# Graph layer, sums by destination: one 112-node window per chunk becomes two 64-node windows, one for each part of 13 and 12 tiles, with weights read 128 columns wide

## The chip, the cores and the metric

The kernel runs on one core of one Trainium2 chip. The metric is the device time of one execution in microseconds (us). Smaller is better. Engine names below are those of the profile: PE is TensorE's matmul, PEld its weight load, DVE is VectorE, ACT is ScalarE, POOL is GpSimd, SP is SyncE, whose queue (SPq) issues most of the transfers.

## The reference

There are 12,500 nodes with 16 features and 400,000 edges, sorted by destination. Each layer adds to x something gathered over the edges, and then normalises:

```python
inv_dx = 1.0 / jnp.maximum(edge_attr_2[:, 0], 1e-6)
slope_e = edge_attr_2[:, 1] * inv_dx
diff = (u[dst] - u[src]) * inv_dx[:, None]
d1 = segment_sum(diff, dst, N) - segment_sum(diff, src, N)
S = segment_sum(broadcast(slope_e, 16), dst, N)
u_next = u - clip(dt, 0.01, 2.0) * (u * d1 + g * S)
x = layernorm(x + u_next)
x = layernorm(x + segment_sum(edge_attr_16, dst, N) / max(count_by_dst, 1))
```

The node ids src and dst are drawn uniformly, and the edges are then sorted by dst, so that a node has 32 edges on the mean (400,000 / 12,500).

## The kernel before, in words

The edges are cut into C = 125 chunks of CH = 3200 edges, each chunk in J = 25 tiles of P = 128 edges. A transfer puts edge 25p + j of a chunk on partition p, as tile j, so that every tile holds edges from the whole of the chunk's span of destinations. That span is about 100 nodes. A window of WIN = 112 nodes from the chunk's least dst holds it. For a chunk with a wider span there is a loop over further windows (`further_in`), which is entered when a table says so; no instruction of its body is in this trace.

Each chunk needs three kinds of TensorE work:

- Sums by src (`tile`, L667 to L678). For every tile the weights are the payload, split in two halves (k) and spread over 8 low positions, and the moving data is a one-hot over 1563 high positions, in four banks (392, 392, 392 and 387 columns). This is 200 matmuls a chunk, L657 and L662, accumulated over all chunks in `ps_src`.
- Rows of x for dst (`take_row`, L599). For every tile one matmul of 48 columns, with the one-hot `node_of_dst` as weights (112 partitions, 128 columns).
- Sums by dst (`take_sum`, L610). For every tile one matmul: weights are the tile's 102 columns of `parts` (3 bf16 parts of 34 values), the moving data is the tile's one-hot of 112 columns, `dst_of_node`, and all 25 accumulate in columns 0 to 111 of `ps_w`.

TensorE runs one stage for each chunk c. Among the matmuls of the 25 tiles of c, the order written by hand puts the rows of x for chunk c + 2 (from tile ROWS_AT = 6, one after each half) and the sums by dst of chunk c + 1 (from tile SUM_AT = 11 to 19, alternately one and two after a half). At tile 11 it waits for `parts_ready`, which DVE gives after L926.

DVE runs one stage for each chunk as well. It opens with `load_stage` (values of the stage's windows from a table into registers) and `add_window` (L962), which waits for the last sum by dst, adds `ps_w` to `dst_sum` at the chunk's base (L971) and copies `dst_rel` to `more_rel` (L972). Then come 25 one-hots of 1564 columns (L1018), and between them the pieces that prepare the next chunk: L929 (`dst_rel2`, the destinations less the chunk's base, doubled), five one-hots of 5 tiles x 112 columns (L939), the arithmetic of the payload (L897 to L926), the spread (L997). One-hots lie in a ring of 13.

ACT builds `node_of_dst` from `rel_all` (L537, L539) and casts. POOL gathers x[src] with one indirect transfer for each tile (L436), paced by TensorE's progress. SP reloads src, dst, the two edge attributes, the window of x and `rel_all` for later chunks, six transfers a stage, each behind a semaphore that frees its buffer.

Before the first stage a prologue finds each chunk's least and greatest dst on DVE (L793, L800), writes the relative destinations to `rel_d` (L798), makes the tables through three small matmuls (L584 to L586), and takes rows and sums of chunk 0 outside the stages. After the last stage the sums are turned and the layers are finished.

Of the kernel before, what the change touches and what calls it, by code (L numbers as in the profile page):

```python
# [5 lines left out]
def gnn_kernel(nc, x, src, dst, edge_attr_16, edge_attr_2, dt_in, g_in, out):  # L6
# [7 lines left out]
    P = 128  # L14
# [14 lines left out]
    WIN = 112  # L29
    SPL = 3  # L30
# [14 lines left out]
    assert NODES <= 1 << 14 and WIN == 16 * 7  # L45
# [6 lines left out]
    src_v = src.rearrange("(c p j) -> c p j", p=P, j=J)  # L52
    dst_v = dst.rearrange("(c p j) -> c p j", p=P, j=J)
    a2_v = edge_attr_2.rearrange("(c p j) t -> c p (j t)", p=P, j=J)
    a16_v = edge_attr_16.rearrange("(c p j) f -> c p (j f)", p=P, j=J)

    ctx = ExitStack()
    with ctx:
# [24 lines left out]
        dst_of_node = dst_hots[:, 0:J * WIN].rearrange("p (j e) -> p j e", j=J)  # L83
# [14 lines left out]
        parts = sb("parts", [P, J, SPL, V], bf16)  # L98
# [25 lines left out]
        more_i = sb("more_i", [P, 2], i32)  # L124
        more_f = sb("more_f", [P, 1], f32)
        base_diag = sb("base_diag", [P, P], f32)
        base_all = sb("base_all", [P, P], f32)
        base_tab = sb("base_tab", [1, P], i32)
        more_tab = sb("more_tab", [1, P], i32)
        stage_tab = sb("stage_tab", [1, (C + 1) * 4], i32)  # L130
# [117 lines left out]
        def later(base, g, first):  # L248

            return nc.s_assert_within(base + (g - first + 1) * WIN, 0, NODES - 1,  # L250
                                      skip_runtime_bounds_check_because="windows are counted up to the one that holds the greatest dst")

        def further_span(eng, c):

            return nc.values_load_multi_w_load_instructions(more_tab[0:1, ds(c, 2)], engines=[eng.engine], min_val=0, max_val=C * (NODES // WIN))[1]

# [56 lines left out]
        A_STEPS, B_STEPS, W_STEPS = 2, 20, 1  # L313
# [8 lines left out]
        def _(sp):  # L322
            def load_src(c, b):
                sp.dma_start(src_i[:, b, :], src_v[ds(c, 1), :, :].rearrange("o p j -> (o p) j")).then_inc(src_loaded[b], 16)

            def load_dst(c, b):
                sp.dma_start(dst_i[:, b, :], dst_v[ds(c, 1), :, :].rearrange("o p j -> (o p) j")).then_inc(dst_loaded[b], 16)

            def load_a2(c, b):
                sp.dma_start(a2[:, b, :], a2_v[ds(c, 1), :, :].rearrange("o p j -> (o p) j")).then_inc(a2_loaded[b], 16)  # L330
# [23 lines left out]
            sp.wait_ge(rel_ready, 1)  # L354
# [64 lines left out]
        def _(pool):  # L419
# [5 lines left out]
            def gather(k, b, pace=None, first=None):  # L425

                pool.wait_ge(src_loaded[b], k * 16 + 16)
# [31 lines left out]
        def _(act):  # L459
# [19 lines left out]
            act.wait_ge(dst_max_ready, 1)  # L479
# [42 lines left out]
            def attr_parts(m, k, b, first=False):  # L522

                act.wait_ge(a16_loaded[b], k * 16 + 16)
# [55 lines left out]
        def _(pe):  # L580
# [4 lines left out]
            nc.tensor.matmul(ps_w[0:1, P:P + C + 1], more_f[0:C, :], before[0:C, 0:C + 1], start=True, stop=True)  # L585
            nc.tensor.matmul(ps_w[:, 2 * P:2 * P + C], ones[0:C, :], base_diag[0:C, 0:C], start=True, stop=True).then_inc(tab_sum, 1)  # L586
# [26 lines left out]
            def sums(hots):  # L613
                for j in range(J):
                    last = take_sum(hots, j)
                return last
# [7 lines left out]
            def further_rows(n):  # L624
# [11 lines left out]
                return span  # L636

            def window_sums(n, span, first=False):

                pe.wait_ge(dst_hot_ready, n + 1)  # L640
                pe.wait_ge(parts_ready, n + 1)
                if not first:
                    pe.wait_ge(win_added, n)
                sums(dst_of_node).then_inc(win_sum_ready, 1)
                further_sums(span)

            def further_sums(span):

                def more(g, first):
                    pe.wait_ge(more_dhot, g + 1)  # L650
                    sums(more_node).then_inc(more_sum, 1)

                further_in(pe, span, more)
# [13 lines left out]
            def tile(c, j, stop, does_sums, does_rows):  # L667
# [4 lines left out]
                for k in range(HLV):  # L672
# [8 lines left out]
                    for s in range((j - SUM_AT) * 3 + first, (j - SUM_AT) * 3 + first + count):  # L681
                        if does_sums and 0 <= s < J:
                            one = take_sum(dst_of_node, s)
# [46 lines left out]
            span = further_rows(0)  # L730
# [3 lines left out]
            window_sums(0, span, first=True)  # L734
# [15 lines left out]
        def _(dve):  # L750
# [7 lines left out]
            def settle(base=0):  # L758
# [15 lines left out]
            step(v.memset(parts[:, :, :, :], 0.0))  # L774
# [18 lines left out]
            step(v.tensor_reduce(lim[0:C, 0:1], dst_all, AX, ALU.min))  # L793
# [4 lines left out]
            v.tensor_scalar(rel_split.rearrange("c (j p) -> c j p", p=P), dst_all.rearrange("c (p j) -> c j p", j=J),  # L798
                            lim[0:C, 0:1], None, ALU.subtract).then_inc(rel_ready, 1)
            v.tensor_reduce(lim[0:C, 1:2], dst_all, AX, ALU.max).then_inc(dst_max_ready, 1)  # L800
            dve.wait_ge(dst_max_ready, 1)
            step(v.tensor_tensor(more_i[0:C, 0:1], lim[0:C, 1:2], lim[0:C, 0:1], ALU.subtract))
            step(v.tensor_scalar(base_diag[0:C, 0:C], ident[0:C, 0:C], lim[0:C, 0:1], None, ALU.mult))
            settle()

            step(v.tensor_single_scalar(more_i[0:C, 1:2], more_i[0:C, 0:1], 4, ALU.arith_shift_right))
            settle()
            step(v.tensor_single_scalar(more_i[0:C, 0:1], more_i[0:C, 1:2], 9363, ALU.mult))
            settle()
            step(v.tensor_single_scalar(more_i[0:C, 1:2], more_i[0:C, 0:1], 16, ALU.arith_shift_right))  # L810
            settle()
            v.tensor_copy(more_f[0:C, :], more_i[0:C, 1:2]).then_inc(tab_sum, 1)
            dve.wait_ge(tab_sum, 2)
            step(v.tensor_copy(base_tab[0:1, 0:C], ps_w[0:1, 0:C]))
            step(v.tensor_copy(more_tab[0:1, 0:C + 1], ps_w[0:1, P:P + C + 1]))
            settle()
            v.tensor_copy(base_all[:, 0:C], ps_w[:, 2 * P:2 * P + C]).then_inc(tables_ready, 1)
            dve.wait_ge(tables_ready, 1)
            by_stage = stage_tab[:, :].rearrange("o (s q) -> o q s", q=4)
            step(v.tensor_copy(by_stage[:, 0, 1:C + 1], more_tab[0:1, 0:C]))  # L820
            step(v.tensor_copy(by_stage[:, 1, 0:C + 1], more_tab[0:1, 0:C + 1]))
            step(v.tensor_copy(by_stage[:, 2, 0:C], more_tab[0:1, 1:C + 1]))
            step(v.tensor_copy(by_stage[:, 3, 1:C + 1], base_tab[0:1, 0:C]))
# [11 lines left out]
            def load_stage(s):  # L835

                before_last, last, after, base = nc.values_load_multi_w_load_instructions(
                    stage_tab[0:1, ds(s * 4, 4)], engines=[dve.engine], min_val=0, max_val=max(C * (NODES // WIN), NODES - 1))[1]
                done["window"] = (before_last, last)
                done["span"] = (last, after)  # L840
                done["base"] = base

            def finish(n, k, b, piece, base_step):
# [36 lines left out]
                if piece == "lo":  # L880
                    if isinstance(n, int) and n == 0:
                        dve.wait_ge(src_loaded[0], 16)
# [294 lines left out]
```

## Time and profile before

| what | value |
|---|---|
| median of 3 runs | 4494.73 us |
| lowest and highest of them | 4491.13 and 4495.12 us |
| the profiled execution's own time | 4491.46 us |
| its span, first to last instruction | 4489.6 us |
| PE busy | 4396.0 us, 98% |
| DVE busy | 3896.7 us, 87% |
| POOL busy | 3316.7 us, 74% |
| ACT busy | 1431.9 us, 32% |
| mean granted clock of TensorE | 0.996 of 2.4 GHz |

The span is the time between the first and the last instruction on the core; the execution's own time is 1.9 us longer. A matmul's busy time in the profile is from its start to the arrival of its last result, and neighbours overlap, so what a matmul costs in a dense stream is read from the distance between starts, not from its own duration. An engine that is not the bound may idle without cost.

### The profile page before, as it was taken

To read this page: it belongs to the slowest core of one execution; us is meant where nothing else is said; L and a number is where in the kernel's file an instruction comes from. 1 tells how busy PE (TensorE), PEld (TensorE's weight loads), DVE (VectorE), ACT (ScalarE), POOL (GpSimd) and SP (SyncE) were. 2 spreads that over 40 slices of the span, in tenths; PEclk is the share of its full clock that TensorE was granted. 3 is DMA by queue.
4 is the path that set the end of the run, shared out by engine and by line. 5 is a ranking of instruction groups with operands and counts; after the bars stand their busy time and mean duration, and the time that the engine had idled before them with its cause. 6 is when DMAs were issued, how large, how long until landed. Compare 5 with 4: busy or idle time off the path is not lost. (4 is left out here: it accounts for less than half of the span.)

```text
span 4489.6 us, 74222 instructions
## 1 busy us (share of the span) xinstructions
PE 4396.0 (98%) x31379; PEld 1159.0 (26%) x12630; DVE 3896.7 (87%) x8730; ACT 1431.9 (32%) x1018; POOL 3316.7 (74%) x3133
## 2 busy tenths in 40 slices
PE   4999999999999999999999999999999999999997
PEld 1222222222222222222222222222222222222222
DVE  7988888888888888888888888888888888888887
ACT  4333333333333333333333333333333333333320
POOL 7777777777777777777777777777777777777760
PEclk9999999999999999999999999999999999999998
DMA  3111111111111111111111111111111111111110
GB/s 94 35 35 35 43 37 35 35 35 42 37 35 35 36 42 37 35 35 41 39 35 35 35 43 37 35 35 35 43 37 35 35 35 42 37 35 35 36 31 8
DMA packets 210292, 167.80 MB, mean 37 GB/s; under 512 B 124651, under 2 KB 193775, under 8 KB 210025
## 3 DMA queue, kind: packets, MB, share of 16 engines
q1 hardware_dynamic: 109798, 139.79, 9.9%
q0 software_dynamic: 100000, 25.80, 6.6%
q10 hardware_dynamic: 476, 2.01, 0.1%
q8 instruction: 7, 0.11, 0.0%
q14 instruction: 11, 0.08, 0.0%
HBM read 164.55 MB, written 2.81 MB: 37 GB/s over the span
## 5 line engine op out<-in xcount | busy, mean ns | idle before, releaser
L662 PE MATMUL ps_src<-hi_hot,spread_lo 128*128 128x392 bf16 (+1 forms) x18750 | 4114.8, 328 | 0.0
L436 POOL DMA_INDIRECT x_src<-in_x_dram,src_i x3125 | 3311.7, 1060 | 1039.9 <-issue 906.0
L1018 DVE TENSOR_SCALAR hi_hot<-col_h,hi_f,scale 128x1564 bf16<-128x1564 f16 x3125 | 2161.3, 711 | 24.4 <-PE ps_src L662 23.2
L657 PE MATMUL ps_src<-hi_hot,spread_lo 128*128 128x392 bf16 x6250 | 2048.4, 328 | 11.4 <-DVE hi_hot L1018 9.3
L657 PEld LDWEIGHTS ps_src<-hi_hot,spread_lo 128*128 128x128 f16 x6250 | 616.0, 99 | 1718.2 <-issue 1383.6
L537 ACT ACTIVATE nodes_mem<-rel_all,row_neg 128x3200 bf16<-128x3200 f16 x125 | 370.3, 2962 | 1507.1 <-PE ps_x L599 1505.0
L610 PEld LDWEIGHTS ps_w<-dst_hots,parts 128*102 128x102 bf16 x3125 | 391.3, 126 | 939.4 <-issue 901.4
L997 DVE TENSOR_TENSOR spread_lo<-spread_lo,halves 128x640 f16<-128x640 f16 x1250 | 603.3, 491 | 12.6 <-PE ps_src L662 12.4
L599 PE MATMUL ps_x<-xwin,nodes_mem 112*128 112x48 bf16 x3125 | 579.9, 188 | 20.4 <-DVE parts L926 13.5
L610 PE MATMUL ps_w<-dst_hots,parts 128*102 128x112 bf16 x3125 | 499.5, 213 | 0.0
L599 PEld LDWEIGHTS ps_x<-xwin,nodes_mem 112*128 112x128 bf16 x3125 | 302.4, 98 | 601.2 <-issue 563.5
L971 DVE TENSOR_TENSOR dst_sum<-dst_sum,ps_w 102x112 f32 x125 | 34.0, 272 | 475.1 <-PE ps_w L610 475.1
L539 ACT ACTIVATE nodes_mem<-nodes_mem,ones 128x3200 bf16<-128x3200 bf16 x125 | 370.3, 2962 | 4.1
L520 ACT COPY spread_lo<-lo_hot 128x3200 f16<-128x3200 f16 x124 | 353.8, 2853 | 0.0
L939 DVE TENSOR_TENSOR dst_hots<-col_h,dst_rel 128x560 bf16<-128x560 f16 x625 | 275.6, 442 | 0.0
L515 ACT CAST halves<-ps_x 128x400 f16<-128x400 f32 x125 | 61.5, 492 | 668.9 <-DVE ps_x L914 668.9
L529 ACT CAST parts<-attr_rest 128x400 bf16<-128x400 f32 x125 | 71.3, 570 | 516.5 <-DVE attr_rest L959 516.5
L830 DVE TENSOR_REDUCE ps_w<-ps_x 128x160 f32<-128x480 f32 x375 | 191.8, 570 | 0.4 <-DVE dst_rel L1005 0.4
L517 ACT CAST parts<-ps_x 128x425 bf16<-128x425 f32 x125 | 68.1, 545 | 126.8 <-DVE ps_x L917 126.8
L511 ACT CAST parts<-ps_w 128x425 bf16<-128x425 f32 x125 | 68.2, 546 | 109.1 <-DVE ps_w L900 109.1
L897 DVE TENSOR_TENSOR ps_w<-ps_w,x_src 128x400 f32<-128x400 f32 x125 | 70.8, 567 | 10.6 <-DMA x_src<-in_x_dram,src_i 10.6
L926 DVE TENSOR_TENSOR parts<-ps_x,parts 128x425 bf16<-128x425 f32 x125 | 75.3, 603 | 4.3
(120 smaller groups left out, 1164.2 us busy)
## 6 DMA issues: line engine op xcount, KB each, us to landing
rel_all<-rel_d SPq DMA_DIRECT2D x125, 800.0 KB
x_src<-in_x_dram,src_i POOLq DMA_INDIRECT x3125
a<-in_edge_attr_dram SPq DMA_DIRECT2D x125, 200.0 KB, 2.4
a<-in_edge_attr_dram SPq DMA_DIRECT2D x125, 25.0 KB
src_i<-in_src_dram SPq DMA_DIRECT2D x125, 12.5 KB, 1.7
dst_i<-in_dst_dram SPq DMA_DIRECT2D x125, 12.5 KB, 1.7
xwin<-xparts_d SPq DMA_DIRECT2D x125, 10.5 KB
dst_sum<-in_dst_dram SPq DMA_DIRECT2D x1, 1400.0 KB
```

Source lines behind the costliest of these rows:

```text
L436: nc.gpsimd.indirect_dma_start(x_src[:, b, j * F:(j + 1) * F], None, x[:, :], bass.IndirectOffsetOnAxis(ap=src_i[:, b, j:j + 1], axis=0)). ...
L520: nc.scalar.copy(lo_rows[:, :, :, :], bc(lo_hot[:, :, :], 3, F)).then_inc(lo_rows_ready, 1)
L537: nc.scalar.activation(node_of_dst[:, :, :], rel_all[:, :, :], ACT.Abs, bias=row_neg[:, 0:1], scale=1.0).then_inc(node_diff_ready, 1)
L539: nc.scalar.activation(node_of_dst[:, :, :], node_of_dst[:, :, :], ACT.Relu, bias=ones[:, 0:1], scale=-1.0).then_inc(node_hot_ready, 1)
L599: return nc.tensor.matmul(ps_x[:, j // PER, (j % PER) * SPL * F:(j % PER + 1) * SPL * F], nodes[0:WIN, j, :], window, start=True, stop=True)
L610: return nc.tensor.matmul(ps_w[0:SPL * V, 0:WIN], parts[:, j, :, :].rearrange("p k v -> p (k v)"), hots[:, j, :], start=(j == 0), stop=(j ...
L657: return nc.tensor.matmul(out_bank, weights, moving, start=False, stop=stop)
L662: return nc.tensor.add_instruction(mybir.InstMatmult(name=nc.get_next_instruction_name(), engine=pe.engine, start_tensor_calc=False, stop_ ...
L830: yield v.tensor_reduce(out_t[:, q * PER:q * PER + n, :], ps_x[:, q, 0:n * SPL * F].rearrange("p (j k f) -> p j f k", k=SPL, f=F), AX, ALU ...
L939: ins = v.tensor_tensor(dst_of_node[:, five, :].rearrange("p j (n t) -> p j n t", t=2), bc(col_h[:, 0:WIN].rearrange("p (n t) -> p n t", t ...
L997: ins = v.tensor_tensor(spread[:, tiles, q, :, :], lo_rows[:, tiles, :, :], bc(halves[:, tiles, q, :], 2, LO), ALU.mult)
L1018: v.tensor_scalar(hi_hot[:, slot(j), 0:HOT], col_h[:, 0:HOT], hi_f[:, b, j:j + 1], scale[:, b, j:j + 1], ALU.is_equal, ALU.mult).then_inc( ...
```

## The change

Edges are laid out differently. A chunk's first 13 x 128 = 1664 edges are part 0 and its last 12 x 128 = 1536 are part 1; within a part of n tiles, edge n·p + j goes to partition p, tile j. So the four loads of a chunk's edge data are two transfers each, and their semaphores count 32 in place of 16. Each part's destinations are counted from the part's own least dst, one-hots by dst have 64 columns in place of 112, and the sums of part 0 go to columns 0 to 63 and of part 1 to columns 64 to 127 of `ps_w`. The weights of a sum are 128 consecutive columns of `parts_mem`, that is the tile's 102 and 26 of what lies behind them; the results of these 26 are not used. DVE adds two windows of 64 in place of one of 112. If a part spans 64 nodes or more, the chunk's further loop runs with destinations outside the parts' windows; it has a table of its own, `sum_tab`.

```diff
+    PWIN = 64
+    JA = 13
+    PARTS = [(0, JA), (JA, J)]
...
+        PARTW = SPL * V
+        parts_mem = sb("parts_mem", [P, J * PARTW + P - PARTW], bf16)
...
             def load_a16(c, b):
-                sp.dma_start(a16[:, b, :], a16_v[ds(c, 1), :, :].rearrange("o p j -> (o p) j")).then_inc(a16_loaded[b], 16)
+                for lo, hi in PARTS:
+                    sp.dma_start(a16[:, b, lo * F:hi * F], part_of(a16_v, c, lo, hi, F)).then_inc(a16_loaded[b], 16)
...
-            def take_sum(hots, j):
-                return nc.tensor.matmul(ps_w[0:SPL * V, 0:WIN], parts[:, j, :, :].rearrange("p k v -> p (k v)"),
-                                        hots[:, j, :], start=(j == 0), stop=(j == J - 1))
+            def part_weights(j):
+                return parts_mem[:, j * PARTW:j * PARTW + P]
+            def take_sum(j):
+                part = int(j >= JA)
+                lo, hi = PARTS[part]
+                return nc.tensor.matmul(ps_w[:, part * PWIN:(part + 1) * PWIN], part_weights(j), dst_of_node[:, j, :],
+                                        start=(j == lo), stop=(j == hi - 1))
...
                 if finish:
-                    span = further_rows(c + 1)
+                    further_rows(c + 1)
+                    span = further_span(pe, c + 1, sum_tab)
...
                 if piece == "rel2":
-                    step(v.tensor_copy(dst_rel2[:, :, :], bc(dst_rel[:, b, :], 2, 2)))
+                    for part, (lo, hi) in enumerate(PARTS):
+                        step(v.tensor_scalar(dst_rel2[:, lo:hi, :], bc(dst_rel[:, b, lo:hi], 2, 2), bases_all[:, 1 + part, ds(n, 1)], None, ALU.subtract))
...
-                win = dst_sum[0:SPL * V, ds(base, WIN)]
-                v.tensor_tensor(win, win, ps_w[0:SPL * V, 0:WIN], ALU.add).then_inc(win_added, 1)
-                step(v.tensor_scalar(more_rel[:, :], dst_rel[:, b, :], 0.0, None, ALU.add))
+                step(v.tensor_tensor(win_a, win_a, ps_w[0:PARTW, 0:PWIN], ALU.add))
+                step(v.tensor_scalar(far[:, :], dst_rel2[:, :, 0], float(PWIN), float(FAR), ALU.is_lt, ALU.mult))
+                dve.wait_ge(dve_step, base_step + count[0])
+                v.tensor_tensor(win_b, win_b, ps_w[0:PARTW, PWIN:2 * PWIN], ALU.add).then_inc(win_added, 1)
+                step(v.tensor_tensor(more_rel[:, :], dst_rel[:, b, :], far[:, :], ALU.add))
```

Besides, `load_stage` takes seven values in place of four. In the prologue the least and the greatest dst are each found for two parts and combined, `rel_split` is written in two instructions, some ten small DVE instructions make the parts' bases and the second table, and the small matmuls that make the tables are more. The initial loads of chunks 0 and 1 are in two transfers each as well, the first of them ahead of `dst_all`, from which the least dst is taken.

## Rows read from the trace of the kernel before

**Rows 1.** The page: busy time and share of PE, and the granted clock in tenths.

```profile
PE 4396.0 (98%) x31379; PEld 1159.0 (26%) x12630; DVE 3896.7 (87%) x8730; ACT 1431.9 (32%) x1018; POOL 3316.7 (74%) x3133
...
PEclk9999999999999999999999999999999999999998
```

**Rows 2.** What PE waited for: us in total, times, longest us.

```profile
PE ps_x L599 <- DVE parts L926: 13.5, 1, 13.5
PE ps_src L657 <- DVE hi_hot L1018: 9.3, 4, 5.8
```

**Rows 3.** Groups by form, PE and PEld: count, busy us, mean ns, idle before.

```profile
L599 PE MATMUL ps_x<-xwin,nodes_mem 112*128 112x48 bf16 x3125 | 579.9, 188 | 20.4 <-DVE parts L926 13.5 <-ACT nodes_mem L539 6.9
L610 PE MATMUL ps_w<-dst_hots,parts 128*102 128x112 bf16 x3125 | 499.5, 213 | 0.0
...
L657 PEld LDWEIGHTS ps_src<-hi_hot,spread_lo 128*128 128x128 f16 x6250 | 616.0, 99 | 1718.2 <-issue 1383.6 <-DVE hi_hot L1018 248.4
L610 PEld LDWEIGHTS ps_w<-dst_hots,parts 128*102 128x102 bf16 x3125 | 391.3, 126 | 939.4 <-issue 901.4
L599 PEld LDWEIGHTS ps_x<-xwin,nodes_mem 112*128 112x128 bf16 x3125 | 302.4, 98 | 601.2 <-issue 563.5
```

**Rows 4.** Timeline of PE, one stage's length: start us, length us, instruction, count.

```profile
2003.65 0.19 PE L599 MATMUL ps_x<-xwin,nodes_mem 112*128 112x48 bf16 x1
...
2010.54 0.21 PE L610 MATMUL ps_w<-dst_hots,parts 128*102 128x112 bf16 x1
...
2011.28 0.26 PE L610 MATMUL ps_w<-dst_hots,parts 128*102 128x112 bf16 x2
...
2021.95 0.26 PE L610 MATMUL ps_w<-dst_hots,parts 128*102 128x112 bf16 x2
...
2023.42 0.33 PE L657 MATMUL ps_src<-hi_hot,spread_lo 128*128 128x392 bf16 x1
...
2038.64 0.19 PE L599 MATMUL ps_x<-xwin,nodes_mem 112*128 112x48 bf16 x1
```

**Rows 5.** Timeline of DVE around a stage's start, idle before in brackets.

```profile
2007.51 0.60 DVE L926 TENSOR_TENSOR parts<-ps_x,parts 128x425 bf16<-128x425 f32 x1
...
2023.06 0.27 DVE L971 TENSOR_TENSOR dst_sum<-dst_sum,ps_w 102x112 f32 x1 [3.80 <-PE ps_w L610]
2023.25 0.17 DVE L972 TENSOR_SCALAR more_rel<-dst_rel 128x25 f32<-128x25 f32 x1
2023.63 1.88 DVE L1018 TENSOR_SCALAR hi_hot<-col_h,hi_f,scale 128x1564 bf16<-128x1564 f16 x3 [0.20 <-PE ps_src L662]
...
2028.40 0.19 DVE L929 CAST dst_rel<-dst_rel 128x50 f16<-128x50 f32 x1
```

**Rows 6.** Timeline of the prologue, several engines.

```profile
0.73 0.41 SPq L324 DMA_DIRECT2D src_i<-in_src_dram  x1
...
13.61 3.49 DVE L793 TENSOR_REDUCE lim<-dst_sum 125x1 f32<-125x3200 int32 x1 [2.90 <-DMA dst_sum<-in_dst_dram]
...
18.74 5.94 DVE L798 TENSOR_SCALAR fin_mem<-dst_sum,lim 125x3200 f16<-125x3200 int32 x1
...
39.63 0.57 DVE L959 TENSOR_TENSOR attr_rest<-a,parts 128x400 f32<-128x400 f32 x1 [6.10 <-ACT parts L527]
...
40.35 1.89 DVE L939 TENSOR_TENSOR dst_hots<-col_h,dst_rel 128x560 bf16<-128x560 f16 x5
...
53.85 1.25 PE L599 MATMUL ps_x<-xwin,nodes_mem 112*128 112x48 bf16 x25 [13.51 <-DVE parts L926]
54.92 2.56 PE L610 MATMUL ps_w<-dst_hots,parts 128*102 128x112 bf16 x25
```

**Rows 7.** POOL's gathers on the page, and their waits for PE.

```profile
L436 POOL DMA_INDIRECT x_src<-in_x_dram,src_i x3125 | 3311.7, 1060 | 1039.9 <-issue 906.0
...
POOL x_src L436 <- PE ps_src L662: 130.3, 239, 3.2
```

**Rows 8.** The longest wait of SP's queue, and one of its transfers.

```profile
SPq L339 <- PE ps_x L599: 1420.6, 124, 21.9
...
2032.04 0.33 SPq L333 DMA_DIRECT2D a<-in_edge_attr_dram  x1
```

More of the change, by code:

```diff
@@ L584, in _ @@
             nc.tensor.matmul(ps_w[0:1, 0:C], lim[0:C, 0:1], ident[0:C, 0:C], start=True, stop=True)
-            nc.tensor.matmul(ps_w[0:1, P:P + C + 1], more_f[0:C, :], before[0:C, 0:C + 1], start=True, stop=True)
-            nc.tensor.matmul(ps_w[:, 2 * P:2 * P + C], ones[0:C, :], base_diag[0:C, 0:C], start=True, stop=True).then_inc(tab_sum, 1)
+            nc.tensor.matmul(ps_w[0:1, P:P + C + 1], more_f[0:C, 0:1], before[0:C, 0:C + 1], start=True, stop=True)
+            nc.tensor.matmul(ps_w[0:1, 2 * P:2 * P + C + 1], more_f[0:C, 1:2], before[0:C, 0:C + 1], start=True, stop=True)
+            for part in range(2):
+                nc.tensor.matmul(ps_x[0:1, 0, part * P:part * P + C], part_lim[0:C, part:part + 1], ident[0:C, 0:C], start=True, stop=True)
+            for t in range(3):
+                last = nc.tensor.matmul(ps_x[:, 1, t * P:t * P + C], ones[0:C, :], base_diag[0:C, t, 0:C], start=True, stop=True)
+            last.then_inc(tab_sum, 1)
             pe.wait_ge(gi_done, 3)
@@ L635, in further_rows, with window_sums_first @@
                 further_in(pe, span, more)
[L636 to L645, printed above, removed]
+            def window_sums_first():
+                pe.wait_ge(dst_hot_ready, 1)
+                pe.wait_ge(parts_ready, 1)
+                for j in range(J):
+                    last = take_sum(j)
+                last.then_inc(win_sum_ready, 1)
+                further_sums(further_span(pe, 0, sum_tab))
             def further_sums(span):
@@ L733, in _ @@
             x_of_dst(1)
-            window_sums(0, span, first=True)
+            window_sums_first()
             with pe.Fori(0, C - 2) as i:
@@ L773, in _ @@
             v.memset(more_rel[:, :], 0.0).then_inc(more_b, 1)
-            step(v.memset(parts[:, :, :, :], 0.0))
+            step(v.memset(parts_mem[:, :], 0.0))
             dve.wait_ge(gi_done, 3)
@@ L792, in _ @@
             dve.wait_ge(dst_all_loaded, 32)
-            step(v.tensor_reduce(lim[0:C, 0:1], dst_all, AX, ALU.min))
+            for part, (lo, hi) in enumerate(PARTS):
+                step(v.tensor_reduce(part_lim[0:C, part:part + 1], dst_all[:, lo * P:hi * P], AX, ALU.min))
+            settle()
+            step(v.tensor_tensor(lim[0:C, 0:1], part_lim[0:C, 0:1], part_lim[0:C, 1:2], ALU.min))
             dve.wait_ge(xrest_ready, 1)
@@ L835, in load_stage @@
             def load_stage(s):
[L837 to L840, printed above, removed]
+                sums_first, sums_last, rows_first, rows_last, base, base_a, base_b = nc.values_load_multi_w_load_instructions(
+                    stage_tab[0:1, ds(s * QS, QS - 1)], engines=[dve.engine], min_val=0, max_val=max(C * (NODES // WIN + 1), NODES - 1))[1]
+                done["window"] = (sums_first, sums_last)
+                done["span"] = (rows_first, rows_last)
                 done["base"] = base
+                done["part_bases"] = (base_a, base_b)
             def finish(n, k, b, piece, base_step):
```

136 lines of the change are left out of this document (86 added, 50 removed).

## The prediction, made before the change was run

> **What bounds the kernel now.** I read the page first. PE is busy 98% of the span at the full granted clock, 2.4 GHz, in all but the ends of it [rows 1]. A busy PE is not yet a PE that sets the time, so the next view is what it waited for. Its two longest waits for DVE in or before the stages are 13.5 us once, in the prologue, and 9.3 us in four pieces [rows 2]. Over 124 stages that is nothing: inside a stage no other engine holds PE. The reader should then see in the timeline of PE that a stage takes 2038.64 - 2003.65 = 34.99 us, and that its matmuls follow each other without a hole [rows 4]. 125 x 34.99 is 4374 us of the 4489.6. So a nanosecond taken out of PE's stream in a stage is a nanosecond of the result, until some other engine becomes the slower one.
>
> **What each kind of matmul costs in the stream.** Durations overlap, so I take distances between starts, over long stretches so that the rounding to 10 ns goes away [rows 4].
> - From 2023.42 to 2038.64 there are only halves of tiles, four wide matmuls each, 23 of them: 15.22 / 23 = 0.6617 us each.
> - From 2003.65 to 2010.54 there are 10 halves with one row matmul (48 columns) each: 6.89 / 10 = 0.689 us. A row matmul costs 27.3 ns.
> - From 2010.54 to 2021.95 there are 15 halves, 15 row matmuls and 22 sums (eight halves with one, seven with two): 11.41 - 15 x 0.6617 - 15 x 0.0273 = 1.075 us, over 22 is 48.8 ns for a sum of 112 columns.
> Check: 50 x 0.6617 + 25 x 0.0273 + 25 x 0.0488 = 34.99 us, the stage. 112 columns at 2.4 GHz are 46.7 ns, so a sum pays for its columns and 2.2 ns more, and its 102-column weight load lies under the neighbours. A row matmul with 48 columns would be 20 + 2.2 = 22.2 ns but costs 27.3, so there is a floor near 27 ns for a pair of load and matmul.
>
> **The change on PE.** A sum has 64 columns: 26.7 + 2.2 = 28.9 ns, just above the row's 27.3. That needs a weight load that fits under 29 ns. The load of 102 columns takes 126 ns from start to end, the 128-column loads of L657 and L599 take 99 and 98 [rows 3]: the wider load is the shorter. If both have the same fixed part, the difference, 27 ns, is in the columns. And the 128-column kind does run at 27.3 ns a pair, in the rows. In the prologue, with PE after a long idle time, 25 rows take (1.25 - 0.19) / 24 = 44 ns each while 25 sums take (2.56 - 0.21) / 24 = 98 ns each [rows 3, 6], which is 112 columns at 1.2 GHz (93 ns) and a little. So I take 29 ns as the price of the new sum. Bounds: 27.3 ns (the row's) from below, 48.8 ns from above if the load stays what a 102-column load may be and only fits under as much as now. A stage has 25 sums, 124 stages have them: 3100 x (48.8 - 29) = 61.4 us saved. At 27.3 it would be 66.7 us; at 48.8 nothing.
>
> The Trainium skill, "TensorE: Matmul & The Clock Gate", sections "Weight-path perf modes" and "Back-to-back issue gap", says that weights are read in the fast way exactly when they are 128 columns and not fp32, and that a matmul of 1 to 64 columns has a floor of about 60 cycles, 25 ns. The 98 and 99 against 126 ns agree with the first, the 27.3 ns of the rows lies 2 ns above the second. By the floor of 25 ns the saving would be 73.8 us. The same page's section "LDWEIGHTS" speaks against the change: a load is put at its columns divided by 1.2 GHz, 107 ns for 128. If that were the slot of a sum, the change would cost 3100 x (107 - 48.8) = 180 us. The trace does not agree: by that rule the 102 columns of now would take 85 ns, and a sum's slot is 48.8.
>
> **PE's other additions.** Two more values are loaded from `sum_tab` in PE's queue at each stage's start. Before, two loads and a branch stand at the same place and there is no hole there: the 23 halves between 2023.42 and 2038.64 include the end of one stage and the start of the next at the same 0.6617 us [rows 4]. The queue runs ahead of the array. I cost it at nothing; cover gone, each 100 ns of hole is 12.4 us.
>
> **DVE.** The window: L971 to L972 is 0.19 us and L972 0.17 [rows 5]. Two adds of 64 for one of 112, one small instruction more and a wait for it: between 0.2 and 0.55 us more, I take 0.35. L929 becomes two: 0.1 to 0.2 more [rows 5]. The five one-hots of 560 elements follow each other at (1.89 - 0.44) / 4 = 0.36 us [rows 6]; with 320 elements at least 0.21, I take 0.24, so 5 x 0.12 = 0.6 us less (between 0 and 0.75). Net about -0.1 us, at worst +0.75. Seven values for four are loaded while DVE idles: it waits 3.80 us for the last sum in every stage [rows 5]. What remains after the stage shrinks by 25 x 19.8 ns = 0.50 us is 3.80 - 0.50 + 0.1 = 3.4 us, at worst 2.5. The point where PE could first feel DVE is tile 11, behind `parts_ready`: L926 ends at 2008.11 and PE gets there at 2010.54, 2.4 us later [rows 4, 5]. No one-hot or payload step moves by more than 0.75 us, so it holds. POOL, ACT and PE behind these DVE steps have the same margins or more. I cost DVE at nothing.
>
> **SP and the transfers.** Ten issues a stage for six, at 0.33 us each: 1.3 us more in a queue that waits 1420.6 us for PE alone, 11.4 us a stage [rows 8]. Every load is for a chunk one to two stages later. Nothing on the path.
>
> **POOL.** This is the engine with the least room. Its own time for 3125 gathers is 3311.7 + 906.0 = 4217.7 us, 33.74 us a chunk, and it waits 130.3 us for PE, 1.04 a chunk [rows 7]. The stage falls to 34.99 - 0.50 = 34.49 us, still 0.75 above POOL.
>
> **Ends of the program.** On the path before the first stage are SP's one extra issue ahead of `dst_all` (0.4 us), L793 and L798 each cut in two with one combining step (0.4), and the window of chunk 0 (0.35) [rows 5, 6]. The small steps for the tables run before 39.63, where DVE has idled 6.10 us for ACT [rows 6]; some ten steps of 0.15 to 0.3 us fit. The 25 sums at the low clock fall from 98 to about 64 / 1.2 + 5 = 58 ns: -1.0 us. At the last stage another 0.3. Together +0.5 us; bounds -1 to +4.
>
> **Sum.** 4491.46 (the profiled execution) - 61.4 + 0.5 = 4430.6 us. The profiled execution lies 3.3 us under the median of the runs shown and near the lowest, so I put 2.4 of it back: **4433 us**, 1.4% less. Its own range is 4426 to 4440. A difference of 0.2%, 9 us, is about what a measurement of this kernel can tell from no change.
>
> **Rivals.**
> 1. The sum costs more than its columns. The 64-column sum gets a slot between 33 and 46 ns because a load cannot be put under so short a neighbour where two sums stand together, or because weights that begin at steps of 204 bytes, as these do, load less well. For it: no 128-column load of this kernel begins off a 256-byte step. Against it: the row's 27.3 ns. At 40 ns: 3100 x 8.8 = 27 us saved, 4467 us. Chance 8%.
> 2. Slower, by one mechanism: the 128-column load of `parts_mem` isn't the fast kind. Then 128 columns at the rate at which the 102 would go through, 53.3 + 2.2 = 55.5 ns, set the slot in place of the 64 columns, 6.7 ns more than now, 3100 x 6.7 = +21 us: 4516 us. It decides as soon as a slot is over 48.8 ns. For it, again the odd start of the weights, and 26 columns that belong to the next tile; against it, 98 and 99 ns for the other two 128-column loads, of both partition counts and both 2-byte types [rows 3]. Chance 6%.
> 3. A new wait in each stage. POOL slows by more than 0.75 us a chunk, since eight loads of 128 short rows share the transfer engines with it where four did, or a changed mix on DVE holds it up, and PE then waits for x[src] through DVE's L897; or PE's queue shows a hole at the stage's start. Half the gain eaten is 0.25 us a stage: 4464 us. Against it: 3.80 us of DVE idle, 0.75 us of POOL room and a buffer of most of a stage between a gather and its reader. Chance 8%, of which 2 in the hundred are so large that the kernel is no faster.
> 4. A part spans 64 nodes or more, so that the further loop runs. A part of 1664 edges at 32 a node spans about 53 nodes, and the spread of that is little over one node. Chance 1%.
>
> **Chances and range.** The forecast has 77%. Faster by over 0.2%: 77 + 8 + 6 = 0.91, less what could lie at the small end, 0.89. Within 0.2%: 0.03. Slower: 0.08 with the second rival, the worst of the third and the fourth. The range for 8 in 10 takes the forecast's own range and the near part of the first and third rivals: 4426 to 4448 us.
>
> **What the profile would show.** L610's starts in a pair 29 ns apart and its loads at 98 ns with 128 columns; a stage of 34.49 us between two like places; DVE's idle before the window add at 3.3 to 3.5 us; POOL's waits for PE down from 130 to about 70 us; PE without waits in the stages; L939 with 320 elements near 0.3 us. It is wrong if a pair of sums stands 33 ns or more apart, if PE waits in every stage, or if loads of `parts_mem` take 126 ns or more.

## The result, and the profile after

The forecast was 4433 us. The changed kernel takes 4585.79 us (median; 4581.80 to 4589.75), the kernel before beside it 4492.47 us: ratio 1.0207, interval 1.0196 to 1.0218. It is slower by 93 us where 59 us less was expected (4492.5 - 4433), so 153 us have to be explained. The chance that I gave to slower was 0.08.

The page after: busy times, the granted clock, the queue that brings instructions (packets, MB, share), and three groups.

```profile
PE 4370.4 (95%) x31389; PEld 1042.3 (23%) x12640; DVE 3847.9 (84%) x9123; ACT 1438.9 (31%) x1018; POOL 3340.3 (73%) x3133
...
PEclk9999999999999999999999999999999999999998
...
q14 instruction: 311, 2.55, 0.2%
...
L641 PEld LDWEIGHTS ps_w<-dst_hots,parts_mem 128*128 128x128 bf16 x3125 | 302.9, 98 | 964.8 <-issue 898.9
...
L641 PE MATMUL ps_w<-dst_hots,parts_mem 128*128 128x64 bf16 x3125 | 436.7, 193 | 0.0
```

The clock is what it was [rows 1], so the loss is not there. PE fell from 98% to 95% of the span, and DVE from 87% to 84%: both idle more. The sum's load takes 98 ns with 128 columns where 102 took 126 [rows 3], as forecast. One line is new in kind. The page before has this one for the same queue:

```profile
q14 instruction: 11, 0.08, 0.0%
```

311 packets against 11 are 300 more, five in each of 60 or so passes through DVE's loop. A pass is one run through the loop's body, which holds two stages.

Timeline of PE after, the 25 sums of a stage (first rows, the last pair, the last):

```profile
2020.65 0.19 PE L641 MATMUL ps_w<-dst_hots,parts_mem 128*128 128x64 bf16 x1
2020.68 0.19 PE L624 MATMUL ps_x<-xwin,nodes_mem 112*128 112x48 bf16 x1
...
2021.37 0.22 PE L641 MATMUL ps_w<-dst_hots,parts_mem 128*128 128x64 bf16 x2
...
2031.62 0.22 PE L641 MATMUL ps_w<-dst_hots,parts_mem 128*128 128x64 bf16 x2
...
2032.35 0.19 PE L641 MATMUL ps_w<-dst_hots,parts_mem 128*128 128x64 bf16 x1
```

The same sum as in the prediction: 2031.62 - 2020.65 = 10.97 us hold 15 halves, 15 rows and 22 sums, so a sum costs (10.97 - 15 x 0.6617 - 15 x 0.0273) / 22 = 28.8 ns. Forecast 29, before 48.8. TensorE's gain is there in full. It is lost again in waits (us in total, times, longest us):

```profile
DVE dst_sum L1028 <- issue: 595.6, 122, 6.5
...
POOL x_src L456 <- PE ps_src L692: 204.8, 248, 3.5
...
PE ps_src L687 <- DVE hi_hot L1078: 68.7, 104, 6.6
...
PE ps_src L687 <- DVE parts_mem L980: 65.6, 82, 1.0
```

PE now waits 134 us for DVE at its matmuls by src (L687), where it was 11.3: the 9.3 of [rows 2] and 2.0 more for L926. DVE's wait before the window add names no engine any more: it was PE [rows 5], now it is "issue", DVE's own queue. Timeline of DVE around three such adds, and the last instruction ahead of the first:

```profile
1993.66 0.19 DVE L1072 TENSOR_TENSOR slope<-a,w 128x25 f32<-128x25 f32 x1
2000.04 0.22 DVE L1028 TENSOR_TENSOR dst_sum<-dst_sum,ps_w 102x64 f32 x1 [6.18 <-issue]
2000.17 0.17 DVE L1029 TENSOR_SCALAR far<-dst_rel 128x25 f32<-128x25 f16 x1
2000.48 0.22 DVE L1031 TENSOR_TENSOR dst_sum<-dst_sum,ps_w 102x64 f32 x1
2000.62 0.18 DVE L1032 TENSOR_TENSOR more_rel<-dst_rel,far 128x25 f32<-128x25 f32 x1
...
2034.86 0.22 DVE L1028 TENSOR_TENSOR dst_sum<-dst_sum,ps_w 102x64 f32 x1 [3.59 <-issue]
...
2072.82 0.22 DVE L1028 TENSOR_TENSOR dst_sum<-dst_sum,ps_w 102x64 f32 x1 [6.49 <-issue]
```

The holes alternate, 6.2 to 6.5 us and 3.6 us. PE's last sum stands at 2032.35 and its result is added only from 2034.86. What fills the holes is in the records of DVE's queue, the loads of `load_stage` above all. (FUSED_REGOPS are operations on the engine's registers; SEQ_ASSERT is the check of a loaded value against its bounds.) First after, then before (count, duration in ns min/median/max, first and last start):

```profile
L890 DVEq FUSED_REGOPS  x1004: 64/183/216, 42.0 to 4494.0; - x168
L890 DVEq SEQ_ASSERT  x882: 23/23/41, 42.3 to 4494.2; - x177
L890 DVEq TENSOR_LOAD <-stage_tab x126: 1024/1037/1298, 40.7 to 4491.3; - x126
```
```profile
L837 DVEq FUSED_REGOPS  x626: 46/183/216, 41.6 to 4395.9; - x157
L837 DVEq SEQ_ASSERT  x504: 23/23/39, 41.9 to 4396.1; - x168
L837 DVEq TENSOR_LOAD <-stage_tab x126: 339/343/603, 41.0 to 4394.7; - x126
```

Four values cost one load of 343 ns, seven cost 1037 ns; each value then goes through a register operation and an assertion on its bounds, 0.28 us from one value to the next. From the load's start to the wait that follows it is 1.51 us before and 3.03 us after (medians over 112 stages or more). And the hole of 6.18 us, put together from single records of the trace (start in us, what starts):

```
1993.75  COMPARE_BRANCH, end of a pass (L1116)
1994.82  packet of 8192 bytes on the instruction queue
1996.60  next instruction of the queue
1996.84  TENSOR_LOAD of seven values
1997.22  packet of 8192 bytes
1999.87  wait for PE's last sum, already there
2000.04  L1028
```

Between the branch and the next instruction lie 2.85 us; before, they are 0.32 us (medians over 61 passes). A packet lands in the middle of it. So the hole is 2.85 us without instructions and 3.0 us of loading, and nothing waits for PE in it.

From these records I also took the room of DVE: the time from the end of the loading to the window add, less the 0.17 us that it takes without any wait. Before: 1.66 and 2.10 us in the two stages of a pass (medians), 3.76 us a pass; by means over the stages it is 3.85. Of the 3.80 us idle that I read [rows 5], only 1.66 us, less than half, was room.

### The profile page after: what moved, and what is told of

Same layout as the page of the kernel before. It is cut to its first block and busy times, and to the rows that moved or that the text cites. A ratio compares the mean times of both kernels' runs of the same rounds, so it can differ in the third digit from the quotient of the medians.

```text
span 4585.7 us, 78030 instructions
## 1 busy us (share of the span) xinstructions
PE 4370.4 (95%) x31389; PEld 1042.3 (23%) x12640; DVE 3847.9 (84%) x9123; ACT 1438.9 (31%) x1018; POOL 3340.3 (73%) x3133
## 5 line engine op out<-in xcount | busy, mean ns | idle before, releaser
L687 PE MATMUL ps_src<-hi_hot,spread_lo 128*128 128x392 bf16 x6250 | 2053.0, 328 | 135.0 <-DVE hi_hot L1078 68.7
L1078 DVE TENSOR_SCALAR hi_hot<-col_h,hi_f,scale 128x1564 bf16<-128x1564 f16 x3125 | 2132.7, 702 | 32.1 <-issue 18.0
L687 PEld LDWEIGHTS ps_src<-hi_hot,spread_lo 128*128 128x128 f16 x6250 | 616.5, 99 | 1879.6 <-issue 1496.4
L1028 DVE TENSOR_TENSOR dst_sum<-dst_sum,ps_w 102x64 f32 x125 | 27.7, 222 | 606.7 <-issue 595.6
L641 PEld LDWEIGHTS ps_w<-dst_hots,parts_mem 128*128 128x128 bf16 x3125 | 302.9, 98 | 964.8 <-issue 898.9
L641 PE MATMUL ps_w<-dst_hots,parts_mem 128*128 128x64 bf16 x3125 | 436.7, 193 | 0.0
L549 ACT CAST parts_mem<-attr_rest 128x400 bf16<-128x400 f32 x125 | 71.5, 572 | 881.5 <-DVE attr_rest L1014 881.5
L994 DVE TENSOR_TENSOR dst_hots<-col_h,dst_rel 128x320 bf16<-128x320 f16 x625 | 195.2, 313 | 0.0
L537 ACT CAST parts_mem<-ps_x 128x425 bf16<-128x425 f32 x125 | 68.2, 545 | 126.8 <-DVE ps_x L971 126.8
L531 ACT CAST parts_mem<-ps_w 128x425 bf16<-128x425 f32 x125 | 68.3, 546 | 93.4 <-DVE ps_w L954 93.4
L547 ACT CAST parts_mem<-a 128x400 bf16<-128x400 f32 x125 | 70.5, 564 | 52.9 <-DVEq L1047 49.8
```

Of the source, the lines that this page charges most:

```text
L641: return nc.tensor.matmul(ps_w[:, part * PWIN:(part + 1) * PWIN], part_weights(j), dst_of_node[:, j, :], start=(j == lo), stop=(j == hi - 1))
L687: return nc.tensor.matmul(out_bank, weights, moving, start=False, stop=stop)
L994: ins = v.tensor_tensor(dst_of_node[:, five, :].rearrange("p j (n t) -> p j n t", t=2), bc(col_h[:, 0:PWIN].rearrange("p (n t) -> p n t", ...
L1078: v.tensor_scalar(hi_hot[:, slot(j), 0:HOT], col_h[:, 0:HOT], hi_f[:, b, j:j + 1], scale[:, b, j:j + 1], ALU.is_equal, ALU.mult).then_inc( ...
```

## The experiments

Two theories stood after the comparison. **Fetch**, theory A in the expectations below: the changed loop of DVE (325 instructions in the built program against 301, and begun at place 146 instead of 121) no longer stays loaded, so each pass fetches it anew; the stall takes about 2.5 us a pass beyond the 0.32, and DVE has not the room for it. My guess at how the place decides was blocks of 128 instructions. **Load**, theory B: seven checked values for four, 1.52 us a stage, are enough by themselves. Theory C puts the loss on the doubled transfers or on PE's queue. That the 128-wide sums cost PE something is ruled out by the slot of 28.8 ns.

The tool to move the loop without changing it is a run of semaphore increments ahead of it, which take up places in the program and nearly no time:

```diff
+        filler = sem("filler")
...
+            for _ in range(60):
+                dve.sem_inc(filler, 1)
             dve.wait_ge(x_loaded, 32)
```

20 in their place were tried in the changed kernel, 45 in the kernel before. The other edit makes the loading cheap, four checked values in one load and the bases unchecked in another (`two_loads`):

```diff
-                sums_first, sums_last, rows_first, rows_last, base, base_a, base_b = nc.values_load_multi_w_load_instructions(
-                    stage_tab[0:1, ds(s * QS, QS - 1)], engines=[dve.engine], min_val=0, max_val=max(C * (NODES // WIN + 1), NODES - 1))[1]
+                sums_first, sums_last, rows_first, rows_last = nc.values_load_multi_w_load_instructions(
+                    stage_tab[0:1, ds(s * QS, 4)], engines=[dve.engine], min_val=0, max_val=C * (NODES // WIN + 1))[1]
+                base, base_a, base_b, _ = nc.values_load_multi_w_load_instructions(
+                    stage_tab[0:1, ds(s * QS + 4, 4)], engines=[dve.engine], min_val=0, max_val=NODES - 1,
+                    skip_runtime_bounds_check_because="they are the least dst of a chunk and of its parts")[1]
```

**First chip.** It ran every kernel 7 to 10% longer, the kernel before at 4926.72 us, with holes in PE's stream in all of them, so its times say little and its traces more.

60 increments, changed kernel:

> The changed kernel with 60 semaphore increments more in DVE's prologue, where DVE idles for a load; nothing else differs. The trace of the changed kernel shows five 8 KB instruction fetches in each pair of stages (300 in all; the kernel before has none in the stages), and DVE's first instruction after the loop's back branch comes 2.85 us after it, in place of 0.32. Theory A: DVE's loop of 325 instructions lies over four blocks of 128 instructions with a fifth fetched ahead, one more than stay resident; moved by 60 it lies over three, the fetches in the stages vanish, a pair of stages falls by 2.5 us from 71.6 to 69.1, and the time is 4430 to 4445 us. Theory B (the seven values and the second window alone made DVE too slow, the fetch only fills a wait): no fetches, but still 4570 to 4590 us. Theory C (the cause is in the doubled transfers or in PE's queue): 4586 us, whether fetches vanish or not.

20 increments, changed kernel:

> The same with 20 increments, the control for the filler itself. Theory A: the loop still lies over four blocks, so the five fetches a pair stay, and so does the time, 4580 to 4592 us. If the filler helps for another reason than where the loop lies, this one is faster too, and the first is no proof. Theories B and C: 4586 us.

45 increments, kernel before:

> The kernel before with 45 increments more in DVE's prologue. Its loop has 301 instructions and lies over three blocks; moved by 45 it should lie over four. Theory A: about five fetches a pair appear, with the 2.5 us behind the back branch. DVE had 1.7 us of true wait in each stage and PE's start of the next stage a further 6 us of one-hots ahead, so the time stays near 4492 us, at most 4505: it is the changed kernel's lack of slack that makes the fetch cost. If fetches do not appear, the block model is wrong. If they appear and the time rises by 100 us or more, the fetch alone is the whole loss.

60 increments and two loads:

> The changed kernel moved by 60, and its seven register values loaded as four with bounds checks and four without, in two loads. Trace: one load of seven takes 1037 ns, one load of four 343 ns, each checked value 0.28 us more; so DVE's loading falls from 3.0 to about 1.9 us a stage. Theory A with PE as the bound again: 4425 to 4438 us, at most 10 us under the changed kernel moved by 60. Theory B: this is the one that returns to about 4430 while the moved one stays at 4586. Theory C: 4586 us.

Measured: 4883.80 us (0.9907, 0.9885 to 0.9929) with 11 packets on the instruction queue; 4916.97 (0.9982) with 311; 4908.50 (0.9962) with 310; 4874.77 (0.9896) with 11. The place of the loop alone makes the fetches come and go, in the kernel before too, and the counts are the same on every chip where a kernel was run again. The times had to be taken elsewhere.

**Second chip**, the kernel before at 4492.12 us.

60 increments, changed kernel:

> The changed kernel moved by 60 instructions of DVE's queue, again, because the chip of the call before ran every kernel, the kernel before too (4926.7 us), some 10% slower, with holes in PE's stream of its own. There the fetches came and went as theory A said (11 against 311), and the moved kernel was 33 us faster than the one moved by 20. On a chip that runs the kernel before at 4492 us: theory A 4430 to 4445 us; theory B (loads and second window alone set the pace) 4570 to 4590 us; theory C 4586 us.

Measured: **4437.41 us** (4434.5 to 4441.8), ratio 0.9875, interval 0.9858 to 0.9893. That is where theory A put it, and it beats both kernels. From its page and its waits:

```profile
PE 4339.9 (98%) x31389; PEld 1044.1 (24%) x12640; DVE 3807.5 (86%) x9123; ACT 1432.2 (32%) x1018; POOL 3362.8 (76%) x3133
...
q14 instruction: 11, 0.09, 0.0%
```
```profile
DVE dst_sum L1031 <- PE ps_w L642: 428.9, 109, 4.4
...
POOL x_src L457 <- PE ps_src L693: 57.7, 177, 4.0
...
PE ps_src L688 <- DVE hi_hot L1081: 13.9, 6, 6.9
...
PE ps_src L688 <- DVE parts_mem L983: 5.3, 10, 1.0
```

With the same instructions in the loop DVE waits for PE again, the branch is 0.33 us long, a stage is 34.49 us, and PE is busy for the whole of three windows of 1000 us (from 1000 to 4000 us). PE's waits at L688 are 19 us in place of 134, and its busy time is 30.5 us shorter (4339.9 against 4370.4): together 146 us, the whole difference of the two spans. The load still takes 1034 ns in the median. So the seven values alone cost no time once PE sets the pace, and the load theory in its strong form falls; theory C, which expected 4586 us, falls with it.

Two loads, the loop not moved:

> The changed kernel with its seven values loaded as four checked and four unchecked, not moved: DVE's loop is 317 instructions from place 140 on and ends 7 behind the place where, by theory A, the fourth block begins. Theory A: five fetches a pair remain, with 2.5 us behind the back branch, and loading falls by about 1.1 us a stage, 2.2 a pair. From 71.6 a pair to 69.4 against PE's 69.0: 4445 to 4470 us. If the fetches are gone, the place of the block's edge is some instructions off, and the time is 4430. Theory B: 4430 to 4450 us with the fetches. Theory C: 4586 us.

Two loads and 60 increments:

> The same moved by 60: both repairs. No fetches, short loads, PE the bound in every stage at 34.49 us: 4425 to 4435 us by theories A and B alike; 4586 us by theory C.

Measured: 4513.25 us (1.0041, 1.0027 to 1.0055), with 10 packets; and 4460.25 us (0.9930, 0.9913 to 0.9948), with 11 packets. Both expectations missed. Theory A expected five fetches a pass in the first, which has none, so the edge of a block is not where I put it; and both are slower than expected, by 43 us or more and by 25. Neither is faster than the dear loads, and in the first something else binds (waits):

```profile
DVE dst_sum L1031 <- PE ps_w L641: 284.1, 115, 3.3
DVE ps_w L954 <- DMA x_src<-in_x_dram,src_i: 254.5, 116, 10.3
...
PE ps_src L687 <- DVE parts_mem L983: 67.7, 96, 1.0
...
POOL x_src L456 <- PE ps_src L692: 32.6, 100, 2.5
```

DVE waits for gathered x[src] in 116 stages. POOL takes 34.87 us for the gathers of a chunk (its busy time and its own issue time, worked out as in the prediction, 3436.9 + 922.3 us over 125), more than the 34.49 us of PE's stage. That is the first mechanism of my third rival. The run at 4437 us has 34.05 us, the one at 4460 us 34.15. The trace of the latter has both conditions in one execution: up to about 1200 us a stage takes 35.3 us and the gathers of a chunk keep POOL busy for 27.6 us, and then, with the same instructions, 34.49 us and 26.9. Its 23 us over the run at 4437 us lie in that first part. Why the gathers are slower in one stretch, or in one program, than in another is open.

**Third chip.** The kernel before ran there at 4994.6 us, with the same kind of holes in all kernels; again only the traces are used.

Two loads and 20 increments:

> The changed kernel with its seven values read by two loads (four checked, three unchecked) and 20 semaphore increments ahead of VectorE's loop, which leave the loop where it is fetched again. Fetch theory (2.5 us of fetch per pass of two stages, and cheaper loads give 2 x about 1.5 us back): about 311 packets on the instruction queue, a pair of stages at 69.4 to 70.5 us, 4445 to 4490 us. Load theory (the seven checked values alone are the loss): the same time as the two-load kernel without fetches, 4513 us or 4460 us, fetches or not. If the fetches cost their full price whatever the loads do: above 4570 us.

45 increments, kernel before:

> The kernel before with 45 semaphore increments ahead of VectorE's loop, nothing else. Fetch theory: about 310 packets on the instruction queue instead of 11, but VectorE has some 1.7 us of real room in a stage there, 3.4 us in a pass, which covers 2.5 us: 4492 us, at most +9 us. If a fetch costs its price whatever the room: 62 x 2.5 = 155 us more, 4647 us. If the moved place does not bring fetches: 11 packets and 4492 us, and the theory of the place is wrong.

Weights 102 wide, 64 columns, 60 increments:

> The changed kernel with 60 increments ahead of the loop (no fetches), its sum's weights read 102 columns wide instead of 128, with 64 columns to multiply as in the change. If the width of the weights sets the rate: weight load back at 126 ns, a slot of 42 to 48 ns instead of 29, 3100 x 0.014 to 0.019 = 43 to 59 us more than 4437, 4480 to 4497 us. If the number of columns alone had set it (128 before, 64 now): 29 ns stay and 4437 us.

Eight values in one load, 60 increments:

> As the changed kernel with 60 increments ahead of the loop, with eight values in the load of a stage instead of seven. If seven values are fetched as 4 + 2 + 1 (three loads of 343 ns), eight go as 4 + 4 or as 8: the load takes 343 or 686 ns instead of 1037 ns, plus 0.28 us for the eighth value's check: time within 5 us of 4437 us. If the price goes by the value: 1150 to 1190 ns.

Ratios 1.0036, 1.0018 and 1.0031, and 5010.41 us for the fourth in its single run; packets 311, 310, 11 and 11. The eight values give a clear answer (queue records):

```profile
L893 DVEq TENSOR_LOAD <-stage_tab x126: 594/598/850, 40.8 to 4914.2; - x126
```

Eight values load in 598 ns, seven in 1037; a price by the value is excluded. 1037 ns is three times 343, as three loads (4 + 2 + 1) would be, but 598 ns is less than twice 343, and neither of the expected 343 or 686. How the values are cut I infer from the durations alone.

**Fourth chip**, the kernel before at 4491.84 us.

Two loads and 20 increments:

> Two loads for seven values, loop left where it is fetched again, once more, on a chip that runs the kernel before in about 4492 us. Fetch theory: 311 packets; VectorE saves 2 x 1.4 us of loading in a pass of two stages, so that 71.6 us become about 69.0 to 70.2 us: 4440 to 4500 us. Load theory: as the two-load kernels without fetches, 4460 to 4513 us. If the fetch costs its full 148 us beside whatever the loads do: 4460 + 148 = 4608 us.

45 increments, kernel before:

> The kernel before with 45 increments ahead of VectorE's loop, once more, on a chip that runs it in about 4492 us. Fetch theory: 310 packets and 4492 us (+9 at most), since 2 x 1.7 us of real room in a pass covers a 2.5 us stall. If a fetch costs its price whatever the room: 4640 us.

20 increments, changed kernel:

> The changed kernel with 20 increments ahead of the loop instead of 60. Place theory: the loop still lies where it is fetched in each pass, 311 packets, and the time of the changed kernel, 4586 us within 10. If the increments ahead of the loop were what helps (by another start of the queues): about 4437 us, or a third of the way, 4536 us.

Weights 102 wide, 64 columns, 60 increments:

> Weights 102 wide with 64 columns and no fetches, once more. The last profile showed the sum's block of 25 at 11.84 us where 128-wide weights gave 11.69 and the kernel before 12.17: 22 slots, so 36 ns for a sum, between 29 and 49. Expected: 4437 + 3100 x 0.007 = 4459 us within 8; if the width is free after all 4437, if it sets all 4490 us.

The last edit, in `part_weights` and `take_sum` (the sum of the further loop, which does not run, is narrowed in the same way):

```diff
-                return parts_mem[:, j * PARTW:j * PARTW + P]
+                return parts_mem[:, j * PARTW:j * PARTW + PARTW]
...
-                return nc.tensor.matmul(ps_w[:, part * PWIN:(part + 1) * PWIN], part_weights(j), dst_of_node[:, j, :],
+                return nc.tensor.matmul(ps_w[0:PARTW, part * PWIN:(part + 1) * PWIN], part_weights(j), dst_of_node[:, j, :],
```

Measured: two loads with fetches 4501.20 us (1.0017, 1.0007 to 1.0026), 1 us above the fetch theory's range and inside the load theory's, so that here only the trace decides; the kernel before with fetches 4494.94 us (1.0007, 0.9997 to 1.0016); 20 increments 4587.91 us (1.0212, 1.0195 to 1.0229); narrow weights 4459.64 us (0.9934, 0.9918 to 0.9949).

The kernel before with its loop moved (page):

```profile
q14 instruction: 310, 2.54, 0.2%
```

It has the fetches, its branch takes 2.95 us instead of 0.32 in the median of 61, and it loses nothing that can be measured. Its room falls from 3.76 to 0.28 us a pass: 3.48 us are eaten, and there they lie beside PE's work. The changed kernel with 20 increments has the fetches and its full loss, so it was the place and not the increments that brought the 148 us back. In the two loads with fetches DVE's window add waits for its own queue in 87 stages, 381.7 us in all, and for gathers DVE waits only twice (14.4 us): what binds there is not what bound in the run at 4513 us.

The table puts the runs in one account. Room is DVE's, per pass, read as above (the sum of two medians); a pass is the mean distance between the first sums by dst of two stages. The kernel before took 4491.8 to 4492.5 us beside every one of them, so that times of different chips may be compared.

| kernel | packets | branch to next, us | loading, us a stage | room, us a pass | pass, us | time, us |
|---|---|---|---|---|---|---|
| before | 11 | 0.32 | 1.51 | 3.76 | 69.91 | 4492.5 |
| before, 45 | 310 | 2.95 | 1.51, 1.89 | 0.28 | 69.93 | 4494.9 |
| changed, 60 | 11 | 0.33 | 3.03 | 0.99 | 69.11 | 4437.4 |
| changed | 311 | 2.85 | 3.03 | 0.36 in the median, PE late | 71.47 | 4585.8 |
| changed, 20 | 311 | 2.87 | 3.03 | 0 | 71.47 | 4587.9 |
| two loads, 20 | 311 | 2.93 | 1.99, 2.38 | 0 | 70.11 | 4501.2 |
| two loads, 60 | 11 | 0.33 | 2.00 | 3.07 | 69.47 | 4460.3 |
| two loads | 10 | 0.29 | 1.99 | 0, POOL late | 70.30 | 4513.3 |

In the kernel before a fetched pass costs DVE 3.48 us. The changed kernel has 0.99 us of room; 3.48 - 0.99 = 2.49 us a pass are left over, 62 of them 154 us, against 4585.8 - 4437.4 = 148 us measured. The closeness is in part chance: with means in place of medians (3.85, 0.34 and 0.86 us of room) it is 2.65 us and 164. Cheap loads return 2 x 1.03 us of room without fetches (3.07 against 0.99), and beside the fetches loading is 1.69 us a pass shorter, the pass 1.36 us and the time 85 us, though the fetches stay. So the loss needs both: the fetch, and the room that was gone. By the same account two loads with fetches should keep 3.48 - 0.99 - 2.06 = 0.4 us of loss a pass, but they are 1.1 us above the 68.97 us of two stages of PE. The other 0.7 us I can't place. Nor does the account cover the two loads that were not fetched where they lie: their 4513 us are POOL's, as said.

The narrow weights: load and first and last sum of one stage.

```profile
L642 PEld LDWEIGHTS ps_w<-dst_hots,parts_mem 128*102 128x102 bf16 x3125 | 392.0, 126 | 935.9 <-issue 898.1
```
```profile
2029.82 0.19 PE L642 MATMUL ps_w<-dst_hots,parts_mem 128*102 128x64 bf16 x1
...
2041.66 0.19 PE L642 MATMUL ps_w<-dst_hots,parts_mem 128*102 128x64 bf16 x1
```

11.84 us for 24 steps, where the wide weights have 2032.35 - 2020.65 = 11.70: 6 ns more for a sum, 35 in place of 29, while the load takes 126 ns in place of 98. So of the 20 ns that a sum gained, the columns give 14 and the width of the weights 6; 3100 x 6 ns = 19 us, and 4459.6 - 4437.4 = 22 us were measured.

## Why the prediction was wrong

**Right.** The sum's slot (29 ns forecast, 28.8 found), the load at 98 ns, the stage of 34.49 us, full clock; rivals 1, 2 and 4 did not occur. With the loop at a place where it isn't fetched, the forecast of 4433 us for the change stands against 4437.4 measured, inside its range of 4426 to 4448. That is in part luck, since DVE's room, held to be 3.4 us a stage, was down to 0.5. SP's ten issues and PE's two more values cost too little to see in that run. POOL's waits for PE, forecast at 70 us, were 57.7 there. The start of the program was dearer than the 0.5 us put on the ends: the profiled execution took 4441.8 us where the sum has 4430.6. In it the first two distances between the stages' first sums were 33.87 and 37.83 us (before, 29.80 and 36.42) and the next nine 34.6 to 35.5, and only then did the stage settle at 34.49.

**The step that failed** is the one for DVE: "Seven values for four are loaded while DVE idles: it waits 3.80 us", and from it "What remains ... is 3.4 us, at worst 2.5" and "I cost DVE at nothing". Three things were wrong in it.
1. 3.80 us of idle were counted as room. The records of the queue, which I did not open for that line, show that the branch and the loading fill half of it: from L1012's end to the wait for PE lie some 2.0 us, and 1.66 us of the stage shown were room. An idle time "<-PE" names what came last, not what filled it. The run of 4437 us shows how little it says: forecast at 3.3 to 3.5 us, the idle before the window add was 3.85 us a stage (428.9 us "<-PE" and 52.7 "<-issue" over 125), no less than before, with 0.5 us of room in it.
2. The seven values were given no price. They cost 1.52 us a stage more. The window was right in size (from L1028's start to L1032's end 0.76 us, against 0.36 from L971 to the end of L972 before: +0.40, forecast 0.2 to 0.55), and so were the one-hots (313 ns each for 441: 5 x 0.13 us less). DVE's busy time fell by 89 us in the run of 4437 us, 0.7 us a stage, more than my 0.1. Room per stage came out at 0.5 us in place of 3.4.
3. The instruction fetch was not in the sum at all. No row of before shows it, because the loop was not fetched there, and 24 more instructions and another start were enough. Cause and price are shown: moving the loop by 60 takes away fetches and 148 us, moving it by 20 leaves both, and in the kernel before, which has 3.76 us of room a pass, fetches cost nothing that can be measured.

The sign that I gave for being wrong, PE waiting in every stage, nearly came: in 125 stages there are 104 waits for L1078 and 82 for L980.

My third rival, a new wait per stage, had the right form, but for POOL and PE's queue and not for DVE's; its POOL side did come up in the runs with two loads. I put 4464 us on it, and two chances in a hundred on no gain. DVE, with 3.80 us of idle time before the window add, was the engine I held to be safe.

The Trainium skill, "Runtime: NRT & Kernel Launch", section "Instruction fetch mechanics", says that a taken branch to a target outside the loaded window forces a transfer of instructions before work goes on. The trace agrees, with 2.85 us at the branch and a packet in them. The same section gives blocks of 16 KiB; here single packets of 8192 bytes come, in the pass shown at 1994.82, 1997.22, 2002.54, 2036.59 and 2058.14 us, and the measurement decides. At which places and lengths a loop is fetched I did not settle by an experiment. In the built programs the loops that were fetched in each pass lie at places 146 to 470, 160 to 476, 166 to 466 and 166 to 490; those that were not, at 121 to 421, 140 to 456, 200 to 516, 206 to 530 and 208 to 536. All nine fit one description: a loop is fetched if it begins ahead of some place between 166 and 200 and also runs past some place between 456 and 466. What lies at these places isn't shown.

## What to carry to other kernels

An engine's idle time ahead of a wait is room only from the moment at which its own queue has reached the wait: look at the queue's loads, register operations and branches before spending it. Compare the packets on the instruction queues before and after any edit that lengthens or moves a loop; if they rise, instructions that do nothing, put ahead of the loop, tell what the fetch costs (here 60 took the fetches away and 20 did not, so try more than one number). Load register values in fours: four took 343 ns and eight 598, but seven 1037.

## What the runs showed of the hardware

- A loop of 325 instructions on VectorE was fetched anew in each pass or never, by its place in the program alone: 311 or 11 packets of 8192 bytes, 2.85 or 0.33 us at the branch, 4585.8 or 4437.4 us.
- One load of four register values took 343 ns, of seven 1037 ns, of eight 598 ns. A checked value cost another 0.28 us.
- With 64 columns to multiply, 128-wide weights gave a slot of 29 ns and 102-wide ones 35 ns, with loads of 98 and 126 ns.
- The indirect gathers of a chunk took POOL 34.05 to 34.87 us in runs of nearly the same program, on the same chip; within one execution its busy time for them fell from 27.6 to 26.9 us a chunk, and the stage from 35.3 to 34.49 us.
